# Gate logits in an attention stage: 8 matmuls turned round into four column groups of TensorE, a ScalarE copy and one summing product

## What is computed

```
x = x + tanh(g_xattn) * conv_layer(ctx, ctx, layernorm(x))
flat_x = layernorm(x).reshape(T, D)              # T = 8192 tokens, D = 1024
gate_logits = flat_x @ gate_w + expert_bias      # gate_w is D x 7
aff = sigmoid(gate_logits)
...                                              # top 2 per token, capacity per expert
x = x + tanh(g_ffn) * (shared expert + kept routed experts, weighted by aff)
```

## Time and profile before

| | |
|---|---|
| median of 3 executions | 4483.66 us (4481.62 to 4486.26) |
| the profiled execution's own time | 4481.13 us |
| its span | 4479.3 us |
| attention stage, about | 13 to 2174 us of the span |
| TensorE matmuls busy | 4365.8 us, 97% |
| VectorE, ScalarE, GpSimd busy | 61%, 33%, 20% |
| granted TensorE clock, mean | 0.991 |

### The profile page before, as it was taken

One profiled execution on the slowest core, in us unless ns is written; L12 is line 12 of the kernel. 1 busy time (PEld: TensorE's weight loads), 2 busy tenths in 40 slices (PEclk: granted clock), 3 DMA queues, 4 the chain that ended last, 5 costly groups with the idle time before them and its releaser, 6 DMA issues.

```text
span 4479.3 us, 71987 instructions
## 1 busy us (share of the span) xinstructions
PE 4365.8 (97%) x27338; PEld 4042.9 (90%) x27338; DVE 2750.8 (61%) x2975; ACT 1461.9 (33%) x1939; POOL 874.5 (20%) x1072
## 2 busy tenths in 40 slices
PE   7999999999999999999689999999999999999998
PEld 7999999999999999999578878888888988988986
DVE  7999999999999999999534343222133233233232
ACT  4455454554554545544211111111121121121120
POOL 1222212212222122122000003443001111111111
PEclk9999999999999999999899999999999999999999
DMA  3333333333333333333722233343254344344332
GB/s 107 114 116 103 109 117 108 112 108 112 117 104 108 116 109 113 106 112 99 126 77 92 78 113 78 111 111 91 81 152 98 75 112 99 75 113 98 75 94 48
DMA packets 227122, 457.67 MB, mean 102 GB/s; under 512 B 41744, under 2 KB 107770, under 8 KB 226998
## 3 DMA queue, kind: packets, MB, share of 16 engines
q1 hardware_dynamic: 200150, 388.45, 30.0%
q0 software_dynamic: 26848, 67.41, 7.4%
HBM read 285.86 MB, written 169.89 MB: 102 GB/s over the span
## 4 chain that ended last, share of the span: by engine, by line
PE 46%; DMA 3%; DVE 1%; issue 1%; ACT 0%; SPq 0%; POOL 0%; DVEq 0%; POOLq 0%; ACTq 0%
PE moe_ps L1462 11%; PE moe_ps L1463 11%; PE moe_ps L1464 10%; PE moe_ps L1480 4%; PE moe_ps L1482 4%; PE moe_ps L1481 4%; PE moe_psT L1451 1%; DMA out<-moe_y,moe_add_i 1%; DMA moe_y<-out 1%; DMA out<-moe_y 1%; DVE moe_zl L1360 1%; ACT moe_zh L1132 0%; DVE moe_y L1387 0%; DVE moe_hid L1373 0%; DMA moe_zin<-zT_d 0%
## 5 line engine op out<-in xcount | busy, mean ns | idle before, releaser
L569 PE MATMUL att_psY<-att_kv_hi,att_tz_hi 128*128 128x288 f32 x4608 | 1393.5, 302 | 30.6 <-DVE att_kv_lo L445 30.6
L570 PE MATMUL att_psY<-att_kv_lo,att_tz_hi 128*128 128x288 f32 x4608 | 1359.4, 295 | 0.0
L571 PE MATMUL att_psY<-att_kv_hi,att_tz_lo 128*128 128x288 f32 x4608 | 1355.9, 294 | 0.0
L1462 PE MATMUL moe_ps<-moe_zh,moe_w1h 128*128 128x512 f32 (+2 forms) x2368 | 860.6, 363 | 33.7 <-DVE moe_zl L1360 21.4
L569 PEld LDWEIGHTS att_psY<-att_kv_hi,att_tz_hi 128*128 128x128 f32 x4608 | 865.4, 188 | 30.6 <-issue 30.6
L571 PEld LDWEIGHTS att_psY<-att_kv_hi,att_tz_lo 128*128 128x128 f32 x4608 | 867.8, 188 | 0.0
L570 PEld LDWEIGHTS att_psY<-att_kv_lo,att_tz_hi 128*128 128x128 f32 x4608 | 867.7, 188 | 0.0
L1463 PE MATMUL moe_ps<-moe_zl,moe_w1h 128*128 128x512 f32 (+2 forms) x2368 | 858.9, 363 | 0.0
L1464 PE MATMUL moe_ps<-moe_zh,moe_w1l 128*128 128x512 f32 (+2 forms) x2368 | 856.6, 362 | 0.0
L1373 DVE TENSOR_TENSOR moe_hid<-moe_ps,moe_act_s 128x512 f32<-128x512 f32 (+2 forms) x148 | 91.7, 620 | 887.5 <-PE moe_ps L1464 859.6
L344 ACT ACTIVATE att_y<-att_psY 128x576 f32<-128x576 f32 x512 | 333.2, 651 | 863.9 <-PE att_psY L571 862.1
(11 more groups left out here) (163 smaller groups left out, 5335.2 us busy)
## 6 DMA issues: line engine op xcount, KB each, us to landing
att_kT<-in_cT SPq DMA_DIRECT2D x64, 512.0 KB, 4.2
att_xn<-in_x SPq DMA_DIRECT2D x64, 512.0 KB, 5.8
att_tz_hi<-filt_hi SPq DMA_DIRECT2D x64, 512.0 KB, 3.7
att_tz_lo<-filt_lo SPq DMA_DIRECT2D x64, 512.0 KB, 4.8
out<-att_x SPq DMA_DIRECT2D x64, 512.0 KB, 4.0
z_d<-att_z SPq DMA_DIRECT2D x64, 512.0 KB, 3.7
zT_d<-att_zT SPq DMA_DIRECT2D x64, 512.0 KB, 4.8
moe_zin<-zT_d SPq DMA_DIRECT2D x64, 512.0 KB
```

Source lines behind the costliest of these rows:

```text
L569: nc.tensor.matmul(acc, tz_hi[u][:, d:d + P], hi, start=(c == 0), stop=False)
L570: nc.tensor.matmul(acc, tz_hi[u][:, d:d + P], lo, start=False, stop=False)
L571: last = nc.tensor.matmul(acc, tz_lo[u][:, d:d + P], hi, start=False, stop=(c == a))
L1462: nc.tensor.matmul(acc, w1h[:, c, cols], zh[:, c, 0:w], start=(c == 0), stop=False)
```

## The change

The gate weights become the stationary operand, padded with zeros from 7 to 32 columns, and zT moves (128 columns). The product of tile t goes to the column group t mod 4 of TensorE, that is, to partitions 32j to 32j+31 of psL, and each group sums two of the eight tiles. ScalarE copies the 128x128 of partial sums (32 rows per group, token in the free direction) into part_s, and one matmul with part_s as stationary operand and `pick` (128x7, ones where row 32j+e meets column e) as moving operand sums the four groups and turns the result back to 128 tokens by 7, in another place of psL. VectorE reads it from there. `gates` stands where it stood; the new `sum_gates` stands after `conv(h,u,2)`, and `gate_parts` on ScalarE after `keys_on`. At the start VectorE clears gate_s, for which SyncE's first load waits, and makes `pick` from the identity. `columns` may overwrite zT once `parts_done` is raised, instead of `l_done`.

```diff
-        gate_s = m.sb("gate_s", [P, NT, E])
+        gate_s = m.sb("gate_s", [P, NT, GQ])
+        part_s = m.sb("part_s", [P, P])
+        pick = m.sb("pick", [P, E])
...
         @block.sync
         def _(sp):
-            sp.dma_start(gate_s[:, :, :], gate_w.rearrange("(c p) e -> p c e", p=P)).then_inc(const, 16)
+            sp.wait_ge(gate_clear, 1)
+            sp.dma_start(gate_s[:, :, 0:E], gate_w.rearrange("(c p) e -> p c e", p=P)).then_inc(const, 16)
...
                 if half == 0:
                     wait(act, zT_out, 16 * h)
-                    wait(act, l_done, h)
+                    wait(act, parts_done, h)
...
+            def gate_parts(h):
+
+                act.wait_ge(parts_done, h + 1)
+                wait(act, l_done, h)
+                nc.scalar.activation(part_s[:, :], psL[:, 0:P], ACT.Copy).then_inc(parts_set, 1)
...
                 if ahead:
                     keys_on(h + 1)
+                if back2:
+                    gate_parts(h - 2)
                 normal_x(h, u)
...
             steady(act, step)
             columns(H - 2, 1)
+            gate_parts(H - 2)
             normal_x1(H - 1)
             columns(H - 1, 0)
             columns(H - 1, 1)
+            gate_parts(H - 1)
...
-                nc.vector.tensor_tensor(logit[:, h, :], psL[:, 0:E], bias[:, :], ALU.add).then_inc(l_set, 1)
+                nc.vector.tensor_tensor(logit[:, h, :], psL[:, L_AT:L_AT + E], bias[:, :], ALU.add).then_inc(l_set, 1)
...
+            nc.vector.memset(gate_s[:, :, :], 0.0).then_inc(gate_clear, 1)
             pairs(0, 0)
             pairs(0, 1)
+            dve.wait_ge(made, 2)
+            dve.sem_inc(passed, 1)
+            nc.vector.tensor_reduce(pick[:, :], ident[:, :].rearrange("p (j e) -> p e j", e=GQ)[:, 0:E, :], AX.X,
+                                    ALU.add).then_inc(picked, 1)
             tell_x(0, 0)
...
             def gates(h):
                 pe.wait_ge(zT_set, 2 * h + 2)
+                wait(pe, parts_set, h)
                 wait(pe, l_set, h)
                 for t in range(NT):
-                    last = nc.tensor.matmul(psL[:, 0:E], zT[:, t, :], gate_s[:, t, :], start=(t == 0), stop=(t == NT - 1))
-                last.then_inc(l_done, 1)
-
+                    j = t % 4
+                    last = nc.tensor.matmul(psL[j * GQ:(j + 1) * GQ, 0:P], gate_s[:, t, :], zT[:, t, :],
+                                            start=(t < 4), stop=(t >= NT - 4))
+                last.then_inc(parts_done, 1)
+
+            def sum_gates(h):
+                pe.wait_ge(parts_set, h + 1)
+                nc.tensor.matmul(psL[:, L_AT:L_AT + E], part_s[:, :], pick[:, :], start=True, stop=True).then_inc(l_done, 1)
...
                 if back2:
                     gates(h - 2)
                 conv(h, u, 2)
+                if back2:
+                    sum_gates(h - 2)
                 turn_x(h, 0)
...
             gates(H - 2)
             turn_o(H - 1, 1)
+            sum_gates(H - 2)
             turn_z(H - 1, 0)
             turn_z(H - 1, 1)
             gates(H - 1)
+            sum_gates(H - 1)
```

More of the change, by code:

```diff
@@ L106, in gated_conv @@
     HALF = L // 2
+    GQ = 32
+    assert E <= GQ and P == 4 * GQ and NT % 4 == 0
     assert B * HD == P and H % 2 == 0 and H >= 6 and HD == 8 and RUN + HD // 2 == PAIRS and HALF == BANK
@@ L176, in gated_conv @@
         z_turned, zT_set = m.sem("z_turned"), m.sem("zT_set")
+        gate_clear, picked = m.sem("gate_clear"), m.sem("picked")
+        parts_done, parts_set = m.sem("parts_done"), m.sem("parts_set")
         l_done, l_set = m.sem("l_done"), m.sem("l_set")
         ROOT = 3
+        L_AT = BANK // 2
         block = ctx.enter_context(nc.Block())
@@ L598, in gates @@
                 pe.wait_ge(zT_set, 2 * h + 2)
+                wait(pe, parts_set, h)
                 wait(pe, l_set, h)
                 for t in range(NT):
-                    last = nc.tensor.matmul(psL[:, 0:E], zT[:, t, :], gate_s[:, t, :], start=(t == 0), stop=(t == NT - 1))
-                last.then_inc(l_done, 1)
+                    j = t % 4
[5 more added lines that the diff above has]
+                nc.tensor.matmul(psL[:, L_AT:L_AT + E], part_s[:, :], pick[:, :], start=True, stop=True).then_inc(l_done, 1)
+            pe.wait_ge(picked, 1)
             pe.wait_ge(made, 2)
```

## The result

| | before | after |
|---|---|---|
| median of 4 runs each, us | 4483.02 (4481.62 to 4486.26) | 4439.34 (4438.08 to 4443.53) |
| ratio, 95% interval | | 0.9905 (0.9893 to 0.9917) |
| profiled execution, its span, us | 4481.13, 4479.3 | 4438.08, 4436.3 |

The change saves 43.7 us, about 1%. It is within 4 us of the case that had been given 0.12, four groups at once and capped by the z cycle, 4443.

A forecast was written before the change was run, and what follows sets the result against it. TensorE was taken to bound the attention stage; 1.78 - 0.96 - 0.24 - 0.25 = 0.33 us saved in each of 62 iterations, 20.5 less 0.6 for start and end, gave 4464 us from a 4483.7 median, range 4440 to 4515.

The forecast's parts named there:

- four groups at once: Rival for the gate block: passes take 0.43 us, 0.86 saved an iteration, cut to 0.67; 4443 us; chance 0.12.
- the z cycle: Attention-stage chain beside TensorE, from turn_o through residual and z to turn_z: no more than 0.67 us an iteration can be gained.
- turning alone gains nothing: Gate block: swapping operands trades a load of 128 columns for a stream of 128 at the same price.
- The block's passes: Gate block on TensorE: 16 passes in 9 steps of 0.107, 0.96 us, between bounds 0.43 and 1.71.
- Edges: Entry and exit of the gate block on TensorE: 0.08 plus one emptying, 0.24 us, between 0.08 and 0.70.
- The sum: The f32 matmul directly before turn_x half 0: 0.25 us an iteration, between 0.21 and 0.29.
- The copy hidden: ScalarE's 128x128 copy from PSUM, say 0.32 us: copy and wait cost nothing, turn_x having 0.9 us to spare.
- the forecast's own sign: The forecast is wrong if, among other signs, TensorE shows a wait anywhere in 130 to 2150 us.
- Start +0.55, end +0.6, last block -0.55: Outside steady running: later first load and reduce, residual's wait at the end, cheaper last block; together +0.6 us.
- the serial figure: Rival for the gate block: groups take turns, 16 passes cost 1.71 us; 4512 us, bounds 4500 to 4543; chance 0.27.
- edges eat it: Rival for the gate block: groups overlap but edges cost 0.4 to 0.7 us, no change, 4484 us; chance 0.19.
- Loads exposed: Rival for the gate block: loads no longer lie beside a matmul, 3.5 us more an iteration, 4700 us; chance 0.04.

The follow-up runs named there:

- full_width: Changed kernel with gate weights padded to 128 stationary columns and no column groups; 4493.49 us, ratio 1.0031 to the kernel before.
- one_group: Changed kernel with all eight gate products sent to column group 0, the other groups staying zero; 4512.95 us, ratio 1.0067 to the kernel before.
- pairs_group: Changed kernel with tile t in group t // 2 instead of t mod 4, so queue neighbours share a group; 4442.06 us, ratio 0.9911 to the kernel before.

## Why the prediction was right or wrong

- **What bounds, and that turning alone gains nothing**: right. The clock stayed at 1.00, and `full_width` and `one_group` gain nothing.
- **The block's passes, 9 steps of 0.107 = 0.96: the step that failed.** The argument was that "the two passes of one matmul share a group and stand next to each other in the queue, so they cannot overlap", and that only neighbours overlap. Passes start in fours, 0.107 apart: 4 steps, 0.43, the lower bound. `pairs_group` refutes the argument itself: with four passes of one group in a row the block is the same. A bound had been worked out from rows and a value between was taken on a picture of an in-order queue for which no row stood. By the ratio for three column tiles in the Trainium skill, "TensorE: Matmul & The Clock Gate", Part 3, the estimate was 0.72; it was nearer, and still short.
- **Edges, 0.24**: 0.34 measured, inside the bounds of 0.08 and 0.70. I counted one emptying; the loads show a gap at each end, and 0.27 of the 0.34 belongs to the column groups.
- **The sum, 0.25**: 0.17, below its lower bound of 0.21: its two passes start 0.13 us apart, as close as conv matmuls.
- **The copy hidden, no wait for xhat**: right, 0.26 us long and 0.69 to spare.
- **The z cycle, at most 0.67 us an iteration**: right; 0.64 (0.62 over 52 iterations). TensorE's own work fell by 0.84 and not by 0.33, so the cap, which the forecast merely passed, became what sets the time. By the forecast's own sign, a wait in 130 to 2150 us, it was wrong; the rival that named `turn_z` waiting for z is what happened.
- **Start +0.55, end +0.6, last block -0.55**: +0.86, +0.3, -1.5. At the start the memset was sized rightly (0.31 for 0.35), and 0.45 that no term had came from the load of kT. The last block carried the error of the passes a second time, at the low clock.
- **Rivals**: the serial figure, 4512, was within 1 us what a kernel without the overlap takes (4512.95), and its terms were near too (2.20 us for block and sum, 2.23 measured); "edges eat it" had a true mechanism at 0.34 instead of 0.4 to 0.7. Loads exposed: 0.38 us for all 16, nothing exposed.
- **The range** ended at 4440, on the four-at-once case with the smaller edge. Against that case's 4443 the last block gave 1.0 more, the cap took 62 x 0.03 = 1.9 back, and the expert stage gave 3.6 that no step of the prediction covers. That the time came out below 4440 and not above it is that stage's chance; that it came out near 4443 and not 4464 is the passes.

## What to carry to other kernels

When an array is mostly idle in a block of small matmuls, the bound "all groups at once" deserves the chance that its lack of a counter-row gives it; a value between two bounds needs a row too, not a picture of the queue. Work out the next cycle's slack before the change, as done here with z: it gave the measured gain to 0.05 us an iteration even though the term before it was wrong, and it tells what to move next (here z's transposes by 12 matmuls, 13 us at the stage's end). And try the disputed saving with the suspected cap out of the way on both sides, before and after: only that pair separates what a change saves from what the program lets through.

## What was not expected of the hardware

- Float32 matmuls on four column groups of 32 gave 1.71 / 0.43 = 4.0 times on the passes, in both orders of the groups that were tried; with edges 2.06 / 0.77 = 2.7 times on the block.
- Going into column groups and back cost 0.27 us per block at full clock, with only 0.43 us of passes between; the block of 8 passes had the same edges, 0.54 - 0.21 = 0.33.
- A GpSimd operation on 128x1 values took 0.19 us when it started with a two-input VectorE operation of 2.3 us or 0.01 to 0.03 us before it, and 2.4 to 2.6 us when VectorE's had started 0.03 to 0.17 us earlier. That took back 2.3 of the 2.55 us by which a reordering had moved VectorE's own work forward.
